# Moving the dense stage's first normalisation, its turns, its f16 halves and its weight splits into the attention ahead of it

## The reference, cut to what matters

```
# first attention: 16 heads of 8, blocks of 64 that see themselves and the block before
h   = ln(x; ln1_g, ln1_b)
q, k, v = split(h @ w_qkv + b_qkv)
x1  = x + softmax(mask(q k^T / sqrt(8))) v @ w_out + b_out
# dense stage, part "m": its feed-forward, 128 -> 512 -> 128
h2  = ln(x1; ln2_g, ln2_b)
m   = gelu(h2 @ w1 + b1) @ w2 + b2
xa  = layernorm(x + x1 + m)
# dense stage, part "e": eight experts over all tokens, gated by a threshold
y_e = gelu_tanh(xa @ w1_e + b1_e) @ w2_e + b2_e
out = layernorm(xa + sum_e y_e * gate_e)
```

## Time and profile before

| | us |
|---|---|
| three runs | 1061.83, 1062.89, 1063.31 (median 1062.89) |
| profiled execution, its own span | 1062.5 |
| PE busy | 944.1 (89%) |
| DVE busy | 859.6 (81%) |
| ACT busy | 756.3 (71%) |
| POOL busy | 405.7 (38%) |

### The profile page before, as it was taken

How to read it: one execution, slowest core, us unless ns; L and a number is a source line. 1 busy time by engine, 2 the same in 40 slices (tenths; PEclk the granted TensorE clock), 3 DMA queues, 4 the chain that set the end, 5 groups by cost and what they waited for, 6 DMA issues and landing times. The chain is left out here.

```text
span 1062.5 us, 28952 instructions
## 1 busy us (share of the span) xinstructions
PE 944.1 (89%) x10222; PEld 607.5 (57%) x10222; DVE 859.6 (81%) x2328; ACT 756.3 (71%) x1476; POOL 405.7 (38%) x568
## 2 busy tenths in 40 slices
PE   5999999994889999999999999678888874899996
PEld 3788888872445444444444444246666653788862
DVE  4988988845888999868899999848888866888854
ACT  2666666645889888888888878346767653688854
POOL 3544444443354100000000000023478867676653
PEclk9999999967899999999999999969999985999998
DMA  8333333000002200032212222010111102232318
GB/s 268 123 107 107 107 106 108 24 3 20 1 6 74 72 1 1 1 104 70 77 71 75 87 66 74 20 53 22 32 52 51 54 27 74 75 86 82 85 45 221
DMA packets 61005, 72.60 MB, mean 68 GB/s; under 512 B 8875, under 2 KB 37805, under 8 KB 60865
## 3 DMA queue, kind: packets, MB, share of 16 engines
q1 hardware_dynamic: 50080, 59.36, 17.9%
q0 software_dynamic: 4544, 8.60, 2.4%
q10 hardware_dynamic: 6240, 2.79, 1.1%
HBM read 40.14 MB, written 31.49 MB: 67 GB/s over the span
## 5 line engine op out<-in xcount | busy, mean ns | idle before, releaser
L808 ACT ACTIVATE d__hf<-d__HB,dense__d 128x512 f32<-128x512 f32 x288 | 184.7, 679 | 39.2 <-PE d__HB L1047 38.2
L867 DVE TENSOR_TENSOR d__hl<-d__hf,d__hh 128x1024 f16<-128x1024 f32 x144 | 173.6, 1219 | 20.4 <-ACT d__hh L813 18.1
L813 ACT ACTIVATE d__hh<-d__hf 128x1024 f16<-128x1024 f32 x144 | 152.2, 1057 | 4.6
L781 POOL TENSOR_SCALAR d__rstd<-d__mv 128x4 f32<-128x4 f32 x16 | 14.2, 886 | 353.6 <-DVE d__mv L990 353.6
L1045 PE MATMUL d__YB<-d__hh,d__w2h 128*128 128x512 f16 x288 | 110.5, 384 | 2.5 <-DVE d__tmp L924 2.5
L1046 PE MATMUL d__HB<-d__xl,d__w1h 128*128 128x512 f16 x288 | 110.9, 385 | 0.0
L1045 PE MATMUL d__HB<-d__xh,d__w1h 128*128 128x512 f16 x288 | 110.8, 385 | 0.0
L1047 PE MATMUL d__HB<-d__xh,d__w1l 128*128 128x512 f16 x288 | 110.6, 384 | 0.0
L316 POOL TENSOR_SCALAR_AFFINE_SELECT a__pt<-a__pt 128x512 f32<-128x512 f32 x128 | 81.3, 657 | 75.4 <-ACT a__pt L364 75.3
L1046 PE MATMUL d__YB<-d__hl,d__w2h 128*128 128x512 f16 x288 | 110.1, 382 | 0.0
L1047 PE MATMUL d__YB<-d__hh,d__w2l 128*128 128x512 f16 x288 | 109.9, 382 | 0.0
(11 more groups left out here) (402 smaller groups left out, 2544.4 us busy)
## 6 DMA issues: line engine op xcount, KB each, us to landing
rows<-a__blank SPq DMA_DIRECT2D x72, 268.0 KB, 3.2
d__G<-gates SPq DMA_DIRECT2D x64, 256.0 KB, 3.2
c__xin<-rows SPq DMA_DIRECT2D x39, 134.0 KB, 2.2
dense__stage<-e_w SPq DMA_DIRECT2D x16, 256.0 KB, 3.1
b__stage<-e_w SPq DMA_DIRECT2D x32, 128.0 KB, 2.2
c__yb<-parts SPq DMA_DIRECT2D x8, 256.0 KB, 8.4
c__yb<-parts ACTq DMA_DIRECT2D x8, 256.0 KB, 8.9
out<-c__xo SPq DMA_DIRECT2D x8, 256.0 KB, 2.3
```

What stands on the lines that cost most here:

```text
L808: act.activation(hf[:, q, f], HB[:, f], gelu, scale=1.0 / WS, bias=b1[:, at:at + 1]).then_inc(s_["h_free"], 1)
L813: act.activation(hh[:, j % (LEAD + 1), f - 1:f + 1], hf[:, q, f - 1:f + 1], ACT.Copy).then_inc(s_["hi_done"], 1)
L867: dve.tensor_tensor(hl[:, p, f], hf[:, q, f], hh[:, p, f], ALU.subtract).then_inc(s_["lo%d_done" % i], 1)
```

## The change

For the first 14 of the 16 chunks of 256 tokens (seven of the eight m chunks) the preparation moves into the attention, five or six steps behind the chunk's start:

- "stats" in step s covers x of chunk s and x1 of chunk s - 5 together (four statistics, four aggregations, a power four wide);
- POOL makes the shift -mean * rstd (two instructions on two columns), ACT the normalised rows hn2 ("norm2", two instructions), PE turns them into the free half of WB just ahead of "output", ACT makes h2 and xh and POOL xl ("halves2");
- the weight sets are split in 18 cuts of 512 columns, one a step from step 2 on: ACT scales a cut in place and makes its high half ("split"), POOL makes the low half one step later ("wlow");
- SP fetches the sets 2 to 8 between the blank stores, each behind a wait for the low halves that free its place;
- a last ACT instruction of the attention on scrap data uses Gelu.

`dense_0` keeps the preparation of its last chunk, run at its start beside the first hidden job; its loop starts at step -2, without the weight splits.

```diff
 PARTS_0 = [
     [("scores", 2, 0), ("vproj", 2, 0), ("shift", 3, 1), ("lift", 1, 0), ("weights", 3, 0), ("values", 4, 3),
-     ("copy", 4, 1)],
+     ("copy", 4, 1), ("wlow", 0, 0)],
     [("scores", 2, 1), ("mpad", 2, 0), ("qk", 1, 0), ("output", 5, 0), ("back", 4, 1), ("low", 1, 0),
-     ("weights", 3, 1), ("values", 3, 0)],
+     ("weights", 3, 1), ("values", 3, 0), ("halves2", 6, 0)],
     [("scores", 2, 2), ("proj", 1, 0), ("proj", 1, 1), ("shift", 2, 0), ("stats", 0, 0),
      ("weights", 3, 2), ("values", 3, 1), ("copy", 3, 0)],
     [("scores", 2, 3), ("mpad", 2, 1), ("proj", 1, 2), ("proj", 1, 3), ("back", 3, 0), ("norm", 0, 0),
-     ("weights", 3, 3), ("values", 3, 2)]]
+     ("weights", 3, 3), ("values", 3, 2), ("norm2", 5, 0), ("split", 0, 0)]]
 STAGES_0 = 6
+AHEAD = NB - 2
+CUTS = 2 * (E + 1)
...
+                elif what in ("stats", "norm"):
+                    if s < AHEAD + 5:
+                        step(what, s, k)
+                elif what in ("halves2", "norm2"):
+                    if 0 <= s - stage < AHEAD:
+                        step(what, s - stage, k)
+                elif what == "split":
+                    if 0 <= s - 2 < CUTS:
+                        step(what, s - 2, k)
+                elif what == "wlow":
+                    if 0 <= s - 3 < CUTS:
+                        step(what, s - 3, k)
...
+                if i % 10 == 0 and i >= 20:
+                    sp.wait_ge(w_low, i // 5 - 2)
+                    keep["fetch_set"](sp, i // 10)
...
+                t.link(pool.tensor_scalar(rstd[:, v], mv[:, v, 1], EPS, 1.0, ALU.add, ALU.mult))
+                pool.tensor_tensor(rstd[:, v], rstd[:, v], half[:, v], ALU.pow).then_inc(rstd_done, 1)
...
+                if what == "norm" and n >= 5:
+                    pool.wait_ge(rstd_done, n + 1)
+                    pool.tensor_scalar(shift2[:], mv[:, 2:4, 0], -1.0, 1.0, ALU.mult, ALU.mult).then_inc(shift2_own, 1)
+                    pool.wait_ge(shift2_own, n - 4)
+                    pool.tensor_tensor(shift2[:], shift2[:], rstd[:, 2:4], ALU.mult).then_inc(shift2_done, 1)
+                if what == "halves2":
+                    pool.wait_ge(xh_done, n + 1)
+                    pool.tensor_tensor(xl[:, toks2(n)], h2[:], xh[:, toks2(n)], ALU.subtract).then_inc(xl_done, 1)
+                if what == "wlow":
+                    pool.wait_ge(w_high, n + 1)
+                    pool.tensor_tensor(cut_of(("w1l", "w2l"), n), stage[:, n // 2 % 2, n % 2],
+                                       cut_of(("w1h", "w2h"), n), ALU.subtract).then_inc(w_low, 1)
...
+                if what == "norm2":
+                    act.wait_ge(shift2_done, n + 1)
+                    wait(act, out_full, n + 1 if n else 0)
+                    for a in range(2):
+                        ins = act.activation(hn2[:, a, :], keep["x1"][:, 2 * n + a, :], ACT.Identity,
+                                             scale=rstd[:, 2 + a:3 + a], bias=shift2[:, a:a + 1])
+                    ins.then_inc(norm2_done, 1)
+                if what == "halves2":
+                    if n == 0:
+                        act.wait_ge(keep["d32_in"], 16)
+                    act.wait_ge(x1_own, n + 2)
+                    wait(act, xl_done, n)
+                    act.activation(h2[:], WB[:, TB:2 * TB], ACT.Identity, scale=cols2[:, 0:1],
+                                   bias=cols2[:, 1:2]).then_inc(h2_done, 1)
+                    act.wait_ge(h2_done, n + 1)
+                    act.activation(xh[:, toks2(n)], h2[:], ACT.Copy).then_inc(xh_done, 1)
+                if what == "split":
+                    j, a = n // 2, n % 2
+                    act.wait_ge(keep["wl%d" % (j % 2)], 32 * (j // 2 + 1))
+                    v = stage[:, j % 2, a]
+                    act.activation(v, v, ACT.Copy, scale=WS).then_inc(scaled, 1)
+                    act.wait_ge(scaled, n + 1)
+                    act.activation(cut_of(("w1h", "w2h"), n), v, ACT.Copy).then_inc(w_high, 1)
...
+            act.activation(scrap[:], half[:, 0:2], ACT.Gelu).then_inc(warm, 1)
...
+                    lns = range(4)[both_norms(n)]
+                    if n < NB:
+                        rows_landed(dve, n)
+                    for a in lns:
+                        v = x[:, 2 * n + a, :] if a < 2 else keep["x1"][:, 2 * (n - 5) + a - 2, :]
+                        sums.inc(dve.bn_stats(st[:, a, :], v))
+                    sums.wait()
...
+                    if 0 < n <= AHEAD:
+                        pe.wait_ge(norm2_done, n)
+                        wait(pe, h2_done, n - 1)
+                        for a in range(2):
+                            pe.transpose(WB[:, TB + a * P:TB + (a + 1) * P], hn2[:, a, :], ident[:])
...
-BEGIN, END = -LEAD - 3, JOBS + 3
+BEGIN, END = -LEAD, JOBS + 3
+LAST = M_JOBS - 1
...
-        if 0 <= s + LEAD + 2 < M_JOBS:
-            right.append(("lift", s + LEAD + 2))
+        if s == BEGIN:
+            right.append(("lift", LAST))
...
-                if 0 <= s + LEAD - 5 < E:
-                    split(s + LEAD - 4)
```

More of the change, by code:

```diff
@@ L190, in attention_0 @@
         x = m.sb("x", [P, NT, C])
[L191 to L194, removed]
+        st = m.sb("st", [P, 4, 6])
+        mv = m.sb("mv", [P, 4, 2])
+        half = m.sb("half", [P, 4])
+        rstd = m.sb("rstd", [P, 4])
+        shift2 = m.sb("shift2", [P, 2])
+        hn2 = m.sb("hn2", [P, 2, C])
+        h2 = m.sb("h2", [P, TB])
         hn = m.sb("hn", [P, 2, C])
@@ L304, in step @@
                     power(n)
-                if what == "norm":
+                if what == "norm" and n >= 5:
[10 more added lines that the diff above has]
+                                       cut_of(("w1h", "w2h"), n), ALU.subtract).then_inc(w_low, 1)
+                if what == "norm" and n < NB:
                     rows_landed(pool, n)
@@ L328, in _ @@
             act.wait_ge(half_set, 1)
-            act.activation(scrap[:], half[:], ACT.Exp).then_inc(warm, 1)
+            act.activation(scrap[:], half[:, 0:2], ACT.Exp).then_inc(warm, 1)
             act.wait_ge(first_in, 32)
@@ L388, in step @@
                 if what == "stats":
-                    rows_landed(dve, n)
                     wait(dve, rstd_done, n)
[L392 to L395, removed]
+                    wait(dve, shift2_done, n - 5)
+                    lns = range(4)[both_norms(n)]
[5 more added lines that the diff above has]
+                    sums.wait()
                     settle(dve, passed_dve)
-                    t.inc(dve.bn_aggr(mv[:, 0, :], st[:, 0, :]))
-                    dve.bn_aggr(mv[:, 1, :], st[:, 1, :]).then_inc(var_done, 1)
-                if what == "norm":
+                    for a in lns:
+                        ins = dve.bn_aggr(mv[:, a, :], st[:, a, :])
+                        ins.then_inc(var_done, 1) if a == lns[-1] else sums.inc(ins)
+                if what == "norm" and n < NB:
                     wait(dve, lift_full, n)
@@ L829, in _ @@
                                    bias=cols[:, 2:3]).then_inc(s_["yf%d" % (c % 2)], 1)
[L830 to L833, removed]
+                if 0 <= s + LEAD < JOBS:
+                    hidden(s + LEAD)
+                if s == BEGIN:
+                    right_full(act, "lift", LAST)
                     act.activation(h2[:], QB[:], ACT.Identity, scale=cols[:, 0:1],
                                    bias=cols[:, 1:2]).then_inc(s_["qb_free"], 1)
[L836 to L841, removed]
+                    act.wait_ge(s_["qb_free"], right[("lift", LAST)] + 1)
+                    act.activation(xh[:, toks(LAST)], h2[:], ACT.Copy).then_inc(s_["xh0_done"], 1)
                 c = s - 2
@@ L942, in whole_low @@
             def whole_low(s):
-                return M_JOBS <= s + LEAD + 3 and s - 1 < M_JOBS
+                return s - 1 < M_JOBS
+            for a in range(4):
+                first.inc(dve.bn_stats(st0[:, a, :], x1[:, 4 * LAST + a, :]))
+            first.wait()
+            settle(dve, s_["passed_dve"])
+            for a in range(4):
+                ins = dve.bn_aggr(mv0[:, a, :], st0[:, a, :])
+                ins.then_inc(s_["var0_done"], 1) if a == 3 else first.inc(ins)
+            dve.tensor_scalar(b2s[:], b2, WS, None, ALU.mult).then_inc(s_["b2_done"], 1)
+            dve.wait_ge(s_["rstd0_done"], 1)
+            for a in range(4):
+                ins = dve.tensor_scalar(hn[:, a, :], x1[:, 4 * LAST + a, :], mv0[:, a, 0:1], rstd0[:, a:a + 1],
+                                        ALU.subtract, ALU.mult)
+                ins.then_inc(s_["hn_done"], 1) if a == 3 else first.inc(ins)
             closed = 0
             for s in range(BEGIN, END):
[L947 to L955, removed]
                 if 0 <= s + LEAD - 1 < JOBS and s <= CLOSING and not whole_low(s - 1):
@@ L1109, in _ @@
                     ins.then_inc(s_["pb_full"], 1)
[L1110 to L1113 removed]
+                if s == BEGIN:
+                    pe.wait_ge(s_["hn_done"], 1)
```

104 lines of the change are left out of this document (43 added, 61 removed).

## The result

The changed kernel takes 1056.26 us (median of five runs, 1053.61 to 1058.76); the kernel before, run beside it, 1063.31 (1061.83 to 1067.71). The ratio is 0.9929 with a 95% interval of 0.9903 to 0.9955. The profiled executions span 1053.4 after and 1062.5 before.

The account below looks back on a forecast made before the run. PE, in a circle with DVE, POOL and ACT, was taken to bound the attention; 109.1 us of dense opening could shrink. Sum: 1062.5 + 2.4 + 22.5 + 3.5 - 27 = 1063.9, so 1064 us; range 1048 to 1078.

Parts of the forecast that it names:

- Dense opening: Dense stage's start up to hidden job 12: job 0 starts at once, 81.5 us instead of 108.9, -27 us.
- Rival 3: Dense opening keeps its pace, turns still waiting for DVE; 1071 us, chance 0.10.
- Statistics and power, 0.9 a step: Attention steps 5 to 15: more statistics and a wider power delay the select behind them, 0.9 us a step.
- The failed step: Attention steps 5 to 15: ACT 0.5 us late, so L432 sits out POOL's weight subtraction, 1.15 us a step.
- Steps 3 to 5: Attention steps 3, 4 and 5: POOL's weight subtraction holds the cast L431, +0.8 us each, 2.4 in all.
- tail: Attention's draining end, 213 to 244.2: ACT's norm2 and split lengthen four steps by 0.9, +3.5 us (0 to 8).
- Rival 1: Attention steps: POOL's lock on DVE costs little, only 0.9 a step and the tail remain; 1049 us, chance 0.25.
- Rival 2: Attention steps: PE's longer waits lower the clock, 1.1 us a step, 12 in all; 1076 us, chance 0.20.
- the 3 us that the rule would have added: Attention steps: residual add L458 colliding with POOL's next select, about 0.3 us a step, 1067; left out of the sum.

Follow-up runs that it names:

- e6: Kernel before with only the normalisation, turns and halves moved into the attention, the weights' splits staying in the dense stage; 1052.64 us, ratio 0.9899.
- e1: Changed kernel with POOL's subtraction of the weights' low half moved to the end of a step's last part; 1043.17 us, ratio 0.9827.
- e3: Changed kernel with POOL's shift put behind its two adds of the residual instead of ahead of them; 1071.14 us, ratio 1.0077.
- e9: Changed kernel with POOL's shift behind the residual's adds and the weights' subtraction at the end of the last part; 1047.0 us, ratio 0.9826.
- e4: Changed kernel with the weights' subtraction at the end of the last part and POOL's power behind the select of weights 3,2; 1032.69 us, ratio 0.9720.
- e5: Kernel before the change with its two-row power on POOL moved behind the select of weights 3,2; 1060.01 us, ratio 0.9968.
- e2: Changed kernel with POOL's power of four rows moved behind the select of weights 3,2; 1043.29 us, ratio 0.9813.

## Why the prediction was wrong

- *Dense opening.* Right: -28.7 against -27. Job 0 starts at once, turns are 7.33 apart, and the entry was 1.9 us shorter than reckoned (the second normalisation of chunk 0 began 18.7 behind the start instead of 19.5, and its turn came 6.2 later instead of 7.2). The stage starts at 264.76 and not at 272.8, since the attention grew by 20.2 and not by 28.4. Rival 3 did not come.
- *Statistics and power, 0.9 a step.* The mechanism was right: the select stands behind the power, and the stretch from projection to scores is 0.91 longer. But the next stretch, scores to scores, is 3.31 instead of 3.48, so that the net price is 0.74, as e6 (0.72) and e1 (0.74) show on their own; the prediction had no term for this gain. Of 11 x 0.9 = 9.9 us, 1.8 was too much.
- *The failed step:* "about 0.5 late at L336, so the selects of 190.25 and wlow are 0.5 late too ... and L432, which waits for L431, sits out the whole 1.15". The prediction names no order for the shift and the adds, but its 0.5 comes out only if POOL makes the shift behind its two adds of the residual (0.87 us at 158.11); with that order e3 has ACT 0.6 late. In the code of the changed kernel the shift comes first, within the same item "norm". ACT is in time to 0.04 us, and the subtraction holds the cast, as in steps 3 to 5, and not L432: 0.78 a step instead of 1.15, 4.1 us too much over 11 steps. e3, which has the order that I had assumed, shows the described collision; e9 shows that it is the collision, and not ACT's lateness by itself, that costs. With both prices the 11 steps come to 11 x 1.49 = 16.4 instead of 22.5, and this is what turned the sign.
- *Steps 3 to 5* were right in their sum (2.3 against 2.4), which is in part luck: the three grew by 1.25, 0.30 and 0.77, not by 0.8 each. The *tail* cost 1.6 instead of 3.5, within its bounds. Its part 242.00 to 264.50 ran at a mean granted clock of 0.75, where 0.62 stood in the last 22.2 us before. Which part of the 1.6 is ACT's and which the clock's was not taken apart.
- *Rival 1* (the lock costs little, 1049) was too cheap: the hold was there. *Rival 2* did not come: PE waits 0.86 us for the low halves and 0.57 for the select, and the clock of the loop stays at 1.00. In e3, with 1.64, it fell.
- The rule of the Trainium skill's "GPSIMD Engine Reference" (Specifications) that was set aside, contention for DVE instructions with two SBUF inputs, is borne out by e3: the residual add took 0.89 beside a select and 0.42 elsewhere. In the changed kernel that add started at 164.82, ahead of the select at 165.11, so the 3 us that the rule would have added were not paid.

## What to carry to other kernels

Work moved to an idle engine is priced by what it stands ahead of in that engine's order, and beside which instruction of its neighbour it falls; here two edits of the order alone took the change from 1056 to 1033 us. Read the order inside one item from the code, line by line, before adding up a chain: one pair of lines the other way round was worth some 15 us (1071 against 1056). And take the parts of a change apart before keeping them: the normalisation alone was no slower than the whole, and the weights paid only once their subtraction had another place.

## What was not expected of the hardware

Which of DVE's instructions POOL holds depends on what they read and on what POOL runs. Three that work between SBUF tiles were held beside a select or the weights' subtraction: the cast (0.20 to 0.98), the subtraction behind it (0.23 to 1.12), the residual add L543 (0.42 to 0.89). Those that read a bank that PE writes (WB, MI) ran at their own length beside the same subtraction in e4: L503 (0.68), which began ahead of it, and L524 (0.41), which lies inside it. The Trainium skill's "SBUF — State Buffer" (Who interferes with whom) says that a DVE instruction with at most one SBUF input, outside the two-port modes, does not contend; these two rows agree. By that rule e1's place can be picked from the operands. The cast has one SBUF input too and was held, so by the rule it would have to run in a two-port mode; no row shows the mode.

Not every pair of instructions between SBUF tiles collides, as two observations show. DVE's aggregation of the statistics, from one SBUF tile to another, takes 0.38 us inside a select in e4, as it does at 154.32 in the changed kernel, where POOL is idle:

```profile
154.91 1.27 POOL L371 TENSOR_SCALAR_AFFINE_SELECT a__pt<-a__pt 128x512 f32<-128x512 f32 x2 [1.13 <-ACT a__pt L419]
155.16 0.38 DVE L483 BATCH_NORM_AGGREGATE a__mv<-a__st 128x2 f32<-128x6 f32 x4
```

And POOL's power did not hold the cast: inside it the cast takes 0.20 in e5 (155.60), and the same in e1, e2, e4 and the changed kernel, where the power is four wide and lasts 1.02. No run here shows what sets the power apart from the select and the subtraction.
